# Gather passes of a four-layer graph network on one core: PE's step groups and SP's tile relays as engine loops

## What is computed

```python
edge_index = jnp.stack([src, dst])
x = _layernorm(x + _L0_gnn_ref(x, edge_index))        # sum of x[dst]*norm into src
x = _layernorm(x + _L1_gnn_ref(x, W, edge_index, edge_type_8, 50000, 50000))
                                                      # sum of (x @ W[rel])[src] into dst
x = _layernorm(x + _L2_gnn_ref(x, src, dst, edge_weight1, ...))
                                                      # an MLP per edge, summed into src, an MLP per node
x = _layernorm(x + _L3_gnn_ref(x, edge_index, ...))   # two graph convolutions src -> dst, loops added
```

## Time and profile before

| | us |
|---|---|
| timed runs, median of 3 | 6556.67 (6533.79 to 6564.7) |
| profiled execution | 6601.09, its span 6599.3 |
| PE busy in the span | 4016.7 (61%) |
| POOL busy | 2863.7 (43%) |
| DVE busy | 2306.5 (35%) |
| L1020, matmuls of the four gather passes | 1413.7 busy, 1081.2 idle before them |
| L898, gathers with `y` by `index_D` (e3, e4) | 741.5 busy, 633.6 idle before them |

### The profile page before, as it was taken

How to read it: one execution, slowest core, us unless ns; L and a number is a source line. 1 busy time by engine, 2 the same in 40 slices (tenths; PEclk the granted TensorE clock), 3 DMA queues, 4 the chain that set the end, 5 groups by cost and what they waited for, 6 DMA issues and landing times. The chain is left out here.

```text
span 6599.3 us, 74663 instructions
## 1 busy us (share of the span) xinstructions
PE 4016.7 (61%) x20669; PEld 3196.6 (48%) x20669; DVE 2306.5 (35%) x4709; ACT 1303.5 (20%) x2394; POOL 2863.7 (43%) x2799
## 2 busy tenths in 40 slices
PE   2333362567666642666189888878971668616687
PEld 2112111566422222666189555676751558416686
DVE  6444491234565620114511011243540113401136
ACT  0000000001343410001111222344530001300025
POOL 0655506664366666660400566000126661266602
PEclk9656575555666765555555888999985555755569
DMA  2000041111455531113633333363431112511136
GB/s 96 2 2 2 11 139 32 39 44 41 154 211 205 214 107 29 45 46 133 241 103 106 90 86 89 125 185 142 180 123 25 45 45 84 198 29 45 45 114 227
DMA packets 236073, 639.42 MB, mean 97 GB/s; under 512 B 75772, under 2 KB 77025, under 8 KB 220247
## 3 DMA queue, kind: packets, MB, share of 16 engines
q1 hardware_dynamic: 95223, 478.17, 20.1%
q0 software_dynamic: 87808, 66.01, 5.5%
q10 hardware_dynamic: 52704, 90.93, 3.7%
HBM read 324.53 MB, written 323.19 MB: 98 GB/s over the span
## 5 line engine op out<-in xcount | busy, mean ns | idle before, releaser
L1020 PE MATMUL e_ring<-e_msgs,e_hot 128*128 x6272 | 1413.7, 414 | 1081.2 <-issue 1064.8
L1020 PEld LDWEIGHTS e_ring<-e_msgs,e_hot 128*128 128x128 f32 x6272 | 1381.2, 329 | 1116.6 <-issue 1116.3
L898 POOL DMA_INDIRECT e_msgs<-y,index_D x784 | 741.5, 946 | 633.6 <-issue 453.9
L950 DVE TENSOR_TENSOR e_hot<-e_nodes,keys_D 128x2048 f32<-128x2048 f32 x147 | 336.9, 2292 | 1610.1 <-remote 884.5
L1166 POOL DMA_INDIRECT m_far<-x,index_S x392 | 373.9, 954 | 543.1 <-PE m_p_t L72 356.5
L1058 ACT COPY e_stage<-e_ring 128x512 f32<-128x512 f32 x196 | 114.9, 586 | 2458.3 <-remote 1434.6
L634 POOL DMA_INDIRECT list_D<-d_place,d_target x392 | 448.3, 1144 | 340.6 <-DVEq L588 225.2
L634 POOL DMA_INDIRECT list_S<-s_place,s_target x392 | 387.0, 987 | 436.3 <-DVEq L588 320.9
L898 POOL DMA_INDIRECT e_msgs<-y,index_S x392 | 402.7, 1027 | 364.3 <-DVE index_S L936 177.2
L898 POOL DMA_INDIRECT e_msgs<-x_by_relation,index_D x392 | 374.2, 955 | 214.6 <-issue 112.7
L1320 PE MATMUL m_ring<-m_region,m_hot 128*128 x1568 | 343.3, 423 | 60.5 <-issue 60.5
(11 more groups left out here) (361 smaller groups left out, 6329.6 us busy)
## 6 DMA issues: line engine op xcount, KB each, us to landing
x_by_relation<-d_stage SPq DMA_DIRECT2D x98, 1024.0 KB
agg<-e_stage ACTq DMA_DIRECT2D x196, 256.0 KB
n_in<-agg SPq DMA_DIRECT2D x42, 896.0 KB, 5.5
n_in<-x SPq DMA_DIRECT2D x42, 896.0 KB, 5.3
x<-n_out SPq DMA_DIRECT2D x28, 896.0 KB, 3.6
m_keyrow<-keys_by_step SPq DMA_DIRECT2D x49, 512.0 KB
messages<-m_region SPq DMA_DIRECT2D x98, 256.0 KB
m_region<-messages SPq DMA_DIRECT2D x49, 512.0 KB, 4.0
```

Source lines behind the costliest of these rows:

```text
L898: pool.indirect_dma_start(out=msgs[:, (i % HELD) * D:(i % HELD + 1) * D], out_offset=None, in_=source, in_offset=bass.IndirectOffsetOnAxis ...
L950: nc.vector.tensor_tensor(hot[g % 2][:, :, :], bc(nodes[:, 0:P].unsqueeze(1), [P, GS, P]), bc(order["keys"][:, g * GS:(g + 1) * GS].unsque ...
L1020: mm = nc.tensor.matmul(ring[:, bass.ds(bucket, D)], hot[g % 2][:, k, :], msgs[:, bass.ds(tile, D)], start=False, stop=False, skip_group_c ...
```

## The change

In `stair_pass` two programs are written differently.

SP: the Python loop over 49 batches becomes two loops of the engine, 15 iterations that only relay and 33 that make room and relay, and one relay behind them. The address in `order["used"]` and the value that `s_land` is waited for come from the loop's register. The DMA of `turned` (e0 only) is issued behind the first loop, that is after batch 14, where it was after batch 12.

PE: where there is no `sort` and no `turned` (e1, e3 and e4), the 49 groups become a loop of 24 iterations with two groups in its body, and one group behind it. The table's address and the value of `s_go` come from the loop's register. In e0 the groups stay a Python loop. POOL, DVE and ACT are not touched.

```diff
-            for b in range(BATCHES):
-                if HELD // SLOTS <= b + 1 < BATCHES:
-                    used = sp.value_load(order["used"][0:1, b + 1 - HELD // SLOTS:b + 2 - HELD // SLOTS],
-                                         min_val=1, max_val=GROUPS)
-                    sp.wait_ge(s_group, used)
-                    sp.sem_inc(s_room, 1)
-                for i in range(b * SLOTS, (b + 1) * SLOTS):
-                    sp.wait_ge(s_land[i % SLOTS], before + 16 * (i // SLOTS + 1))
+            def room(b):
+                used = sp.value_load(order["used"][0:1, bass.ds(b + 1 - HELD // SLOTS, 1)], min_val=1, max_val=GROUPS)
+                sp.wait_ge(s_group, used)
+                sp.sem_inc(s_room, 1)
+
+            def relay(b):
+                for r in range(SLOTS):
+                    sp.wait_ge(s_land[r], 16 * b + (before + 16))
                     sp.sem_inc(s_ready, 1)
-                if turned is not None and b == 12:
-                    sp.wait_ge(s_keyt, 2)
-                    sp.dma_start(turned.rearrange("(k s) e -> s k e", k=7), keyt[:, :, :]).then_inc(s_turned, 16)
+
+            full = HELD // SLOTS - 1
+            with sp.Fori(0, full) as b:
+                relay(b)
+            if turned is not None:
+                sp.wait_ge(s_keyt, 2)
+                sp.dma_start(turned.rearrange("(k s) e -> s k e", k=7), keyt[:, :, :]).then_inc(s_turned, 16)
+            with sp.Fori(full, BATCHES - 1) as b:
+                room(b)
+                relay(b)
+            relay(BATCHES - 1)
...
-            for g in range(GROUPS):
+            def group(g, h):
                 _, at = nc.values_load_multi_w_load_instructions(
-                    order["table"][0:1, g * GS:(g + 1) * GS], [mybir.EngineType.PE], min_val=0,
+                    order["table"][0:1, bass.ds(g * GS, GS)], [mybir.EngineType.PE], min_val=0,
...
-                    mm = nc.tensor.matmul(ring[:, bass.ds(bucket, D)], hot[g % 2][:, k, :],
+                    mm = nc.tensor.matmul(ring[:, bass.ds(bucket, D)], hot[h][:, k, :],
...
+            if sort is None and turned is None:
+                with pe.Fori(0, GROUPS // 2) as i:
+                    for h in range(2):
+                        group(i * 2 + h, h)
+                group(GROUPS - 1, 0)
+            else:
+                for g in range(GROUPS):
+                    group(g, g % 2)
```

More of the change, by code:

```diff
@@ L1023, in _ @@
                 mm.then_inc(s_group, 1)
[L1024 to L1036, removed]
+            if sort is None and turned is None:
[6 more added lines that the diff above has]
+                    group(g, g % 2)
+                    if turned is not None and g == 1:
+                        for half, (a, b) in enumerate(((0, 4), (4, 7))):
+                            for k in range(a, b):
+                                mm = flip128(nc, spare[1 + half][0:KS, (k - a) * P:(k - a + 1) * P],
+                                             order["keys"][:, k * KS:(k + 1) * KS], K["ident"][:, :])
+                            mm.then_inc(s_pkeyt, 1)
+                    if sort is not None:
+                        if 4 <= g < 4 + 3 * PARTS and g % 3 == 1:
+                            sort.pe_counts(pe, g // 3 - 1)
+                        if g == 26:
+                            sort.pe_base(pe)
+                        if g == 33:
+                            sort.pe_steps(pe)
         @block.scalar
```

## The result

| | us |
|---|---|
| before, median of 20 runs | 6556.48 |
| after, median of 20 runs | 6577.77 |
| ratio after to before | 1.0036, 95% interval 1.0022 to 1.0050 |
| profiled execution of after | 6572.08, its span 6570.2 |

The forecast was 6055 us; the loops gained nothing and cost some 21 us. The 20 runs of before here have the median that the first three had. The profiled execution of before, 6601, took longer than any of its 20 timed runs, so the two traces are compared stage by stage and not by their ends.

A forecast was written before the change was run, and what follows sets the result against it. 0.70 us slots, blamed on instruction delivery, keep PE behind POOL's gathers; loops gain 462 us in e1, e3, e4 plus 40 in e0, 502 off 6601 gives 6099 profiled, median about 6055; range 5960 to 6760.

The forecast's parts named there:

- What bounds the kernel: Gather passes: 0.70 us slots slow PE and SP; unslowed, e3's 490 us of gathers set the pace, 506 in all.
- Term (3): PE's and SP's loops in e1, e3, e4: looped code escapes the slots, gaining 3 x 154 = 462 us.
- Rival A: PE and SP slots go with issuing, not delivering; added instructions cost 144 to 360 us, 200 taken: 6755 us; chance 0.22.
- D: Rival, PE and SP: slots stay, added instructions fall into the fast stretches, nothing changes, 6540 to 6590 us; chance 0.08.
- Rival B: PE's loop back edges in e1, e3, e4 fetch packets, 76 to 152 us, slots stay: 6670 us; chance 0.08.
- 40 us for SP's loop: In e0, only SP loops; PE freed of SP's share of slots gains between 0 and 100 us, 40 taken.
- The signs: Whole kernel's time: faster by over 0.5% 0.62, same 0.08, slower 0.30.

The follow-up runs named there:

- e0: Not a run: gather pass of the kernel that carries the second sort; the change gave it SP's loop only; 690 us before, 687 after.
- e1, e4: Not a run: gather pass of the kernel with the same gathers and steps as e3; the change gave it PE's and SP's loops.
- e3: Not a run: gather pass of the kernel, the one read in stretches; PE's and SP's loops; 663 us before and after.
- e13: SP's loops alone in all four passes, PE as before, against before, run again on a chip with slots: 1.0014 (0.9998 to 1.0029).

## Why the prediction was wrong

**What bounds the kernel** was read rightly: a pass is POOL-bound in principle at 490 us, and slots of 0.7 us keep PE from keeping up. The chip without slots bears out both numbers, 488 for the gathers and 499 for the pass forecast as 506.

**Term (3) failed**, the step from "slots hit straight-line programs" to "looped code is free of them". In e3's loops, for which q8 brings nothing, PE's branch in the fill phase and SP's relay take 0.7 us, and a pass takes 663 us as before. The trace of before had no loop under unbroken gathers, as I wrote, and I filled the gap with the end that I liked: I took the whole loss for the gain, 462 us, where the measured gain is nothing. Rivals A and D had it right that the slot is not in the delivery. The trace even spoke for it: slots fell on register, semaphore and matmul instructions alike, while a packet of 256 instructions landed in about 1 us.

**Rival A's price failed too.** It multiplied added instructions by 0.70 us and came to 144 to 360 us; the changed kernel lost 21. The price took every instruction added in a slow stretch to cost a slot. In before, register instructions did so to 4992; from 5000 to 5070 they had a median of 0.032 us again, and there "both sequencers get one instruction through per slot" held for loads, matmuls and relays only. For the full ring the likely reason is its rhythm, which no run shows by itself: PE's work is done in the fast stretches, 55 of the 64 matmuls of a cycle in 11.94 us, and what falls into the slow ones displaces little. With a third of PE's instructions gone the time fell 0.3%. The time of "nothing changes" (D, 6540 to 6590) came true; its reason, that the added instructions fall into the fast stretches, was not measured, and the branch at 0.709 us fell into a slow one.

**Rival B did not happen.** PE's back edge has a median of 0.208 us, like the node pass's. The rule of the Trainium skill, "Runtime: NRT & Kernel Launch", instruction fetch mechanics, would have put a fetch at a taken branch that leaves the pages held; in 72 back edges of after none lasts over 0.709 us, which is a slot, and queue q8 moves no packet in e3 from 4905 to 5440. One of the 72 with the stop after 8 lasts 1.243 us. The rule may hold for bodies that are not held; no run here shows it.

**e0** was given 40 us for SP's loop. It took 687 us where it took 690, and with the thinner relay, which takes most of SP's instructions away, 685: PE gains nothing that counts.

**The signs.** 0.62 for faster leaned on one step without a row behind it. The rows could have been asked for a second price: in the full ring PE got 55 matmuls through in 11.94 us and hardly any in the next 10.7, and POOL's stops came to 65.6 us. Of the loss of 154 us the tail (91 us, where the prediction needed 14) makes up 77 and these stops most of the rest: the fill phase builds the tail, and the full ring costs the stops. One sum is off as well: with half of A outside (0.11) and all else inside, the range leaves out 0.11, not 0.15.

## What to carry to other kernels

When two engines lose time to "issue" together, ask first what a third does in those stretches, and change its rhythm before their code; here a shorter lead of POOL (one wait, and the batch that SP reads for it) gained 4.6% where rewriting two engines' programs gained nothing. A producer that is let far ahead of a consumer it disturbs only fills the buffer: let it ahead by what the consumer needs (32 tiles were enough, 128 cost 80 us a pass). And a fixed stop is a bet on the chip: a stop after each 12 gathers costs 5.3% where there are no slots, while a shorter lead should cost nothing there, since PE then stays close (not tried on that chip).

## What the runs showed of the hardware

**Chips differ, by 18% for this kernel.** On three of the four chips that the experiments ran on, gathers that POOL issues every 1.25 us leave PE and SP together about one load, matmul or relay per 0.70 us; on one, used for one group of kernels, they don't. (Whether that is the chip or the time at which it was used, one group can't say.) The chip is not faster as such. The kernel with SP's loops ran on both kinds: the node pass n2 takes 147 us on both, n3 377 and 376, n5 205 and 206, none of them with indirect DMAs, while every stage in which POOL issues them is shorter on the chip without slots, mlp_pass 1082 us in place of 1276. In `order_sources` POOL's scatters first wait 159 us for DVE on both; the other 13 waits occur only with slots (us, times, longest; with slots first):

```profile
POOL list_S L634 <- DVEq L588: 323.1, 14, 158.7
```

```profile
POOL list_S L634 <- DVEq L588: 158.8, 1, 158.8
```

There it is whole pauses of PE, DVE and ACT and not instructions of 0.7 us; whether the cause is the same isn't shown. So a comparison holds only beside before on the same chip.

**What the slots are stays open.** The Trainium skill, "NOTIFIC — the notification-queue block", section 7.1, says that the block which writes the trace's records holds its producers back when its inner queues fill, and that this can stall an engine; every execution here was recorded. What speaks against the sheer number of packets: mlp_pass of before runs with 7513 DMA packets in 100 us, and PE's register instructions are not slowed, while e3 has slots at 3074 packets in 120 us:

```profile
L1388 PEldq ALU_OP  x277: 32/32/32, 4300.1 to 4400.0; - x139
...
DMA packets 7513, 18.30 MB, mean 183 GB/s; under 512 B 832, under 2 KB 832, under 8 KB 7501
```

```profile
DMA packets 3074, 3.18 MB, mean 26 GB/s; under 512 B 1536, under 2 KB 1536, under 8 KB 3072
```

Those 7513 are on other queues than a gather's packets, so records of the gathers' own packets are not ruled out. No execution without a record exists here, so whether the slots are there in one can't be said.

**The clock of the next stage differs from one execution to the next.** With the stop after 10 gathers the node pass n4, which the change does not touch, took longer: from PE's last step of e3 to the first gather of e4 166 us in place of 133. The granted clock, in before, with the stop after 10, and with SP's loops on the chip of e13:

```profile
5600.00:5620.00 20.00, 20.00 (x134) 14.54 (x132) 15.11 (x8) 12.19 (x38) 0.00 (x0) 1.00 0.76 285
```

```profile
5360.00:5380.00 20.00, 20.00 (x75) 14.46 (x76) 9.12 (x5) 6.93 (x22) 0.00 (x0) 0.50 0.61 232
```

```profile
5602.00:5622.00 20.00, 20.00 (x75) 14.36 (x75) 12.12 (x6) 7.14 (x22) 0.00 (x0) 0.50 0.41 161
```

At 0.50, which is 1.2 GHz, PE does 75 matmuls in 20 us, at 1.00, 2.4 GHz, 134. With the stop after 10 the clock rose between 5380 and 5400, over 80 us into n4; before it, PE had only 11 us of work behind the last gather of e3, where before had 100. But that alone does not decide it: with SP's loops PE had been busy for those 100 us as well, the clock rose only some 60 to 80 us into n4, and the stretch took 152 us, while with the stop after 8, where PE had 11 us of work, it took 132. What decides when the clock rises is not shown, and a difference of up to 34 us in one execution's n4 says nothing of a change.
